# A four-stage convolution network: stack copies by quarter, a reordered opening, and six copies on GpSimd's queue

## The reference

```python
x = x + _L0_conv_ref(_gn(x), ...)   # 3x3 convolution, reflected edge; the kernel of each sample is a mix
                                    # of 3 experts, weighted by softmax(mean(_gn(x)) @ fc_w.T + fc_b)
x = x + _L1_conv_ref(_gn(x), ...)   # abs, then a 3x3 convolution per channel, zero edge
x = x + _L2_conv_ref(_gn(x), 8)     # 17x17 box mean, zero edge
x = x + _L3_conv_ref(_gn(x), ...)   # sum of the 8 neighbours, then five 1x1 layers, ELU after four of them
```

## Time and profile before

| | |
|---|---|
| median of 3 runs (lowest to highest) | 706.48 us (704.64 to 708.58) |
| profiled execution, its own time | 707.1 us |
| span of that execution, first to last instruction | 705.2 us |
| PE busy | 603.9 us, 86% of the span |
| DVE busy | 571.1 us, 81% |
| ACT busy | 558.4 us, 79% |
| POOL busy | 321.9 us, 46% |
| DMA | 85.54 MB, mean 121 GB/s |

### The profile page before, as it was taken

One profiled execution on the slowest core, in us unless ns is written; L12 is line 12 of the kernel. 1 busy time (PEld: TensorE's weight loads), 2 busy tenths in 40 slices (PEclk: granted clock), 3 DMA queues, 4 the chain that ended last, 5 costly groups with the idle time before them and its releaser, 6 DMA issues.

```text
span 705.2 us, 13422 instructions
## 1 busy us (share of the span) xinstructions
PE 603.9 (86%) x4142; PEld 167.3 (24%) x4142; DVE 571.1 (81%) x993; ACT 558.4 (79%) x1070; POOL 321.9 (46%) x487
## 2 busy tenths in 40 slices
PE   0547572999999999999999999999999899889995
PEld 0312220222222222222222222222222222222221
DVE  1454763888998899889988998988898779788896
ACT  0223101799999999999999999999999999999995
POOL 2530635146952696078717781579104910450000
PEclk9967886999999999999999999999999999999998
DMA  6779689338577737692869195728540750075001
GB/s 131 170 149 185 126 138 212 76 83 161 114 157 179 152 83 169 150 197 45 193 144 203 26 202 123 158 45 182 132 107 1 156 143 0 1 164 133 16 16 30
DMA packets 74418, 85.54 MB, mean 121 GB/s; under 512 B 9202, under 2 KB 58946, under 8 KB 74370
## 3 DMA queue, kind: packets, MB, share of 16 engines
q1 hardware_dynamic: 65976, 76.82, 50.3%
q10 hardware_dynamic: 8394, 8.12, 5.8%
HBM read 9.14 MB, written 8.39 MB: 25 GB/s over the span
## 4 chain that ended last, share of the span: by engine, by line
PE 46%; DVE 23%; ACT 14%; issue 8%; DMA 5%; SPq 2%; ACTq 1%; POOL 1%; DVEq 1%; POOLq 0%
PE pz L866 21%; PE pc L808 9%; DVE g L1073 8%; PE pc L843 7%; ACT u L719 6%; ACT u L722 5%; DVE bn L1015 4%; DVE g_last L1073 3%; PE po L808 3%; DMA win<-y 3%; PE po L875 2%; PE pz L843 2%; ACT u L725 2%; DVE u L1070 2%; DVE xs L1057 2%
## 5 line engine op out<-in xcount | busy, mean ns | idle before, releaser
L719 ACT ACTIVATE u<-pz 128x512 f32<-128x512 f32 x485 | 267.5, 602 | 67.7 <-PE pz L866 65.4
L866 PE MATMUL pz<-g,wT 64*64 64x512 f32 x1536 | 271.3, 610 | 17.7 <-DVE g L1073 15.7
L1073 DVE SCALAR_TENSOR_TENSOR g<-u,pz 128x512 f32<-128x512 f32 x384 | 246.8, 679 | 45.5 <-ACT u L722 42.1
L722 ACT ACTIVATE u<-u 128x512 f32<-128x512 f32 x485 | 282.6, 640 | 0.9
L866 PEld LDWEIGHTS pz<-g,wT 64*64 64x64 f32 x1536 | 69.3, 131 | 195.5 <-issue 194.1
L1073 DVE SCALAR_TENSOR_TENSOR g_last<-u,pz 128x512 f32<-128x512 f32 x128 | 82.4, 680 | 23.2 <-ACT u L722 22.2
L866 PE MATMUL pz<-stack,wT 64*64 64x512 f32 x512 | 86.3, 619 | 16.1 <-issue 9.6
L843 PE MATMUL pc<-win,t 64*32 64x512 f32 x1344 | 95.0, 639 | 4.9 <-DMA win<-y 2.0
L1015 DVE BATCH_NORM_STATS2 bn<-xs 128x6 f32<-128x512 f32 (+1 forms) x128 | 84.3, 683 | 15.7 <-DMA xs<-in_x_dram 13.1
L808 PE MATMUL pc<-box_sum,box_mat 128*128 128x512 f32 x138 | 74.5, 634 | 1.2 <-DVE box_sum L1089 0.8
L513 POOL TENSOR_TENSOR stat<-stat 128x1 f32<-128x1 f32 x32 | 6.2, 194 | 131.4 <-DVE stat L1030 131.4
(11 more groups left out here) (96 smaller groups left out, 480.5 us busy)
## 6 DMA issues: line engine op xcount, KB each, us to landing
stack<-near_sum SPq DMA_DIRECT2D x93, 192.0 KB, 4.0
win<-y SPq DMA_DIRECT2D x50, 260.0 KB, 4.4
win<-y SPq DMA_DIRECT2D x50, 195.0 KB, 4.4
stack<-box_sum SPq DMA_DIRECT2D x62, 128.0 KB, 3.9
out_dram<-xs SPq DMA_DIRECT2D x7, 1024.0 KB
xs<-in_x_dram SPq DMA_DIRECT2D x5, 1024.0 KB
stack<-near_sum SPq DMA_DIRECT2D x31, 128.0 KB, 2.8
win<-y SPq DMA_DIRECT2D x25, 65.0 KB, 4.5
```

What stands on the lines that cost most here:

```text
L719: act.activation(u[:, m, :], pz[:, m, :], ACT.Relu, scale=-1.0, bias=0.0).then_inc(relu_done, 1)
L722: act.activation(u[:, m, :], u[:, m, :], ACT.Exp, scale=-1.0).then_inc(exp_done, 1)
L866: last = pe.matmul(pz[to, m, :], wT[rows, l, rows], src, start=True, stop=True)
L1073: dve.scalar_tensor_tensor(out=elus(l)[:, m, :], in0=u[:, m, :], scalar=-1.0, in1=pz[:, m, :], op0=ALU.add, op1=ALU.max).then_inc(g_writte ...
```

## The change

The opening is put in another order, and some waits are split.

- The stack of sample 0 goes by quarters (`stack_chunks`, `own_pieces`, `near_pieces`). SP and ACT copy the own rows of quarter 0 as soon as `y3` is written, its neighbour rows after the first neighbour sum, then the own rows of the other three quarters, then the neighbour rows of quarter 1; SP then copies the neighbour rows of the second half. Quarter 0 counts to `stack_first`, the other own rows to `own_first`, the rest to `stack_in`, whose later thresholds become lower by `OWN` or are shifted by it. The layer of quarter 0 waits for `stack_first` alone.
- The first half of sample 2's stage-0 convolution moves on PE from half-step 0 of round 1 to the end of the opening, into `pz[0..1]`, with its evacuation and statistics on DVE; the second half is spread over half-steps 1, 2 and 3, its evacuation moves to half-step 4. The first layer waits for that evacuation.
- Both halves of sample 2's load are issued by SP, after the first windows have landed.
- Sample 1's windows of stage 0: SP copies the upper half after the first half of sample 0's convolution, and the last pieces after the second. The six copies of the lower half are issued by POOL, behind `scales(0, 1)` and ahead of `scales(2, 0)`, and count to `win0_second`. ACT does `normal0(1, c)` ahead of `softmax_exp(1)`.
- DVE does `route_out(0)` ahead of `setup_transposed`.

```diff
win0_in = sem("win0_in")
+        win0_second = sem("win0_second")
...
         stack_in = [sem(f"stack_in{h}") for h in range(2)]
+        stack_first = sem("stack_first")
+        own_first = sem("own_first")
...
         WIN0 = 14 * 16
+        SECOND = 6 * 16
...
         STACK = 14 * 16
+        OWN = 4 * 16
...
-            first = {(0, 0, 1): 2, (0, 1, 0): 0, (1, 0, 1): 2, (1, 1, 0): 2}
+            first = {(0, 0, 1): 2, (0, 1, 0): 0, (1, 0, 1): 2, (1, 1, 0): 2, (2, 0, 0): 0}
...
-        def written(eng, k, h):
-            eng.wait_ge((y0_written, y1_written)[k], (Y0, Y1)[k] // 2 * (h + 1))
+        def windows0_next(eng):
+            eng.wait_ge(conv_mm[0], 1)
+            windows0(eng, 1, (0,), False)
+            eng.wait_ge(y0_written, 2 * Y0)
+            eng.wait_ge(conv_mm[0], 2)
+            for h in range(2):
+                for dst, rows in around(y0, win0, h * K // 2, (h + 1) * K // 2, h, True):
+                    eng.dma_start(dst, rows).then_inc(win0_in, 16)
+        def written(eng, k, h, i=0):
+            n = (Y0, Y1)[k]
+            eng.wait_ge((y0_written, y1_written)[k], n * i + n // 2 * (h + 1))
...
+        def near_pieces(eng, lo, hi, banks, landed):
+            up, down, end = max(lo, 1), lo and lo - (lo > KB), min(hi, K - 1) - (hi == 2 * KB)
+            for m in banks:
+                a, b = max(2 * m - 1, 0), min(2 * m + 3, R)
+                top, bottom = C * (a - 2 * m + 1), C * (b - 2 * m)
+                eng.dma_start(stack[m][top:3 * C, lo:hi], near_sum[C * a:C * (2 * m + 2), lo:hi]).then_inc(landed, 16)
+                eng.dma_start(stack[m][5 * C:5 * C + bottom, lo:hi], near_sum[2 * C * m:C * b, lo:hi]).then_inc(landed, 16)
+            if 0 in banks:
+                eng.dma_start(stack[0][0:C, up:hi], near_sum[7 * C:P, up - 1:hi - 1]).then_inc(landed, 16)
+            if M - 1 in banks:
+                if lo == 0:
+                    eng.wait_ge(near_rows, 2)
+                eng.dma_start(stack[3][7 * C:P, down:end], near_sum[0:C, down + 1:end + 1]).then_inc(landed, 16)
+        def own_pieces(eng, lo, hi, banks, landed):
+            for m in banks:
+                eng.dma_start(stack[m][3 * C:5 * C, lo:hi], y3[2 * C * m:2 * C * m + 2 * C, lo:hi, 1:W + 1]).then_inc(landed, 16)
+        def stack_chunks(eng, banks):
+            eng.wait_ge(y3_written, 4)
+            own_pieces(eng, 0, KB, banks, stack_first)
+            eng.wait_ge(near_rows, 1)
+            near_pieces(eng, 0, KB, banks, stack_first)
+            own_pieces(eng, KB, K, banks, own_first)
+            eng.wait_ge(near_rows, 2)
+            near_pieces(eng, KB, 2 * KB, banks, stack_in[0])
...
             windows_first(sp, 0, 2, True)
-            load_blocks(sp, 2, 0)
-            sp.wait_ge(conv_mm[0], 2)
-            windows0(sp, 1, (0,), True)
+            for h in range(2):
+                sp.wait_ge(win0_first[h], FIRST0)
+            for odd in range(2):
+                load_blocks(sp, 2, odd)
+            windows0_next(sp)
...
             load(3)
-            stacks(sp, 0, 0, (0, 1))
-            stacks(sp, 0, 1, range(M))
+            stack_chunks(sp, (0, 1))
+            sp.wait_ge(near_rows, Q)
+            near_pieces(sp, 2 * KB, K, range(M), stack_in[1])
...
                     pool.wait_ge(norm_step[0], i * NORM + NORM)
-                    pool.wait_ge(win0_in, WIN0 * (i - 1))
+                    pool.wait_ge(win0_in, WIN0 * (i - 1) - SECOND)
...
-                if c == 0:
+                if c == 0 and not (isinstance(i, int) and i == 0):
                     for h in range(2):
-                        pool.wait_ge(stack_in[h], STACK * i)
+                        pool.wait_ge(stack_in[h], STACK * i - OWN)
+                    if isinstance(i, int) and i == 1:
+                        pool.wait_ge(stack_first, STACK)
...
             scales(0, 1)
+            pool.wait_ge(conv_mm[0], 2)
+            written(pool, 0, 1, 1)
+            for dst, rows in around(y0, win0, K // 2, K, 1, False) + [edge0(1)]:
+                pool.dma_start(dst, rows).then_inc(win0_second, 16)
...
                             act.wait_ge(win0_first[h], FIRST0)
-                    elif not (isinstance(i, int) and i == 0):
-                        act.wait_ge(win0_in, WIN0 * (i - 1))
+                    elif isinstance(i, int) and i == 2:
+                        act.wait_ge(win0_in, WIN0 - SECOND)
+                        act.wait_ge(win0_second, SECOND)
...
             windows_first(act, 0, 3, True)
-            load_blocks(act, 2, 1)
-            softmax_exp(1)
...
                 normal0(1, c)
-            act.wait_ge(conv_mm[0], 2)
-            windows0(act, 1, (1,), False)
+            softmax_exp(1)
...
             windows1(act, 1, (1,), False)
-            stacks(act, 0, 0, (2, 3))
+            stack_chunks(act, (2, 3))
...
                             pe.wait_ge(setup_dve, SETUP_DVE)
+                    elif isinstance(i, int) and (i, k, n) == (2, 0, 0):
+                        pe.wait_ge(conv_evac[2], 2)
+                    elif isinstance(i, int) and (i, k, n) == (2, 0, 1):
+                        pe.wait_ge(conv_evac[1], Q * i)
...
                     elif n == 0:
-                        pe.wait_ge((win0_in, win1_in)[k], (WIN0, WIN1)[k] * i)
+                        pe.wait_ge((win0_in, win1_in)[k], (WIN0 * i - SECOND, WIN1 * i)[k])
+                        if isinstance(i, int) and i == 1 and k == 0:
+                            pe.wait_ge(win0_second, SECOND)
...
                         if isinstance(j, int) and j == 0 and q == 0 and m % 2 == 0:
-                            pe.wait_ge(conv_evac[2 - m // 2], (2, Q + 2)[m // 2])
-                        if m == 0 and q < 2:
-                            pe.wait_ge(stack_in[q], STACK * j + STACK)
+                            pe.wait_ge(conv_evac[m // 2], (2 * Q + 2, Q + 2)[m // 2])
+                        if m == 0 and q == 0 and isinstance(j, int) and j == 0:
+                            pe.wait_ge(stack_first, STACK)
+                        elif m == 0 and q == 0:
+                            pe.wait_ge(stack_in[0], STACK * (j + 1) - OWN)
+                        elif m == 0 and q == 1:
+                            if isinstance(j, int) and j == 0:
+                                pe.wait_ge(own_first, OWN)
+                                pe.wait_ge(stack_in[0], STACK - OWN)
+                            pe.wait_ge(stack_in[1], STACK * (j + 1) - OWN)
...
                                     conv_taps(t + 1, 1, n, (kw,))
-                                if first and at in (0, 2):
-                                    conv_taps(t + 1, 0, at // 2, range(3))
+                                if first and at in (1, 2, 3):
+                                    conv_taps(t + 1, 0, 1, (at - 1,))
...
             conv_taps(1, 1, 1, range(3))
+            conv_taps(2, 0, 0, range(3))
...
                         dve.wait_ge(conv_mm[2], Q * i)
-                        for h in range(2):
-                            dve.wait_ge(stack_in[h], STACK * i)
+                        if isinstance(i, int) and i == 1:
+                            dve.wait_ge(stack_first, STACK)
+                            dve.wait_ge(own_first, OWN)
+                        else:
+                            for h in range(2):
+                                dve.wait_ge(stack_in[h], STACK * i - OWN)
...
                 if first:
-                    if at in (0, 2):
-                        evacuate_pair(i, 0, at // 2)
-                    if at in (1, 4):
-                        stats_of(i, 1, (0, 2) if at == 1 else (1, 3))
                     if at == 4:
+                        evacuate_pair(i, 0, 1)
+                        stats_of(i, 1, (1, 3))
...
             setup_natural()
+            route_out(0)
             setup_transposed()
-            route_out(0)
...
             merge_stats(1, 2)
+            evacuate_pair(2, 0, 0)
             group_var(1, 2)
+            stats_of(2, 1, (0, 2))
...
             rounds(dve, one)
```

## The result

| | before | after |
|---|---|---|
| median of 19 runs each (lowest to highest) | 706.48 us (702.87 to 710.62) | 710.86 us (708.32 to 713.46) |
| span of the profiled execution | 705.2 us | 707.7 us |
| ratio of the runs, 95% interval | | 1.0058 (1.0044 to 1.0072) |

The account below looks back on a forecast made before the run. The kernel's end was taken as its pipeline's start plus a constant, so opening time counts. Part 1's 8.9 plus 0.7 for part 2 and Part 3 gave 9.6 off 707.1, 697.5, less 0.6: 696.9 us, range 691 to 702.5.

Parts of the forecast that it names:

- part 2: Opening, first windows and routing: first convolution's second half at 36.35, sample 0's second normalisation 2.34 earlier; with Part 3, 0.7 us.
- The later load of sample 2: Opening: sample 2's load, issued after the first windows land, costs nothing; a landing at 53 would cost three us.
- a gain at the first windows: Sample 0's first convolution: last window copy lands in 3.1 instead of 7.38 us, at 34.3 instead of 38.55.
- Part 3: Six copies on GpSimd, 1.14 us each, end at 53.7; sample 1's convolution at 56.8; with part 2, 0.7 us.
- Copies that land 3.1 after their issue are in by then: Sample 1's window copies land before its convolution starts at 56.8, so they don't hold it.
- the six copies end last: Sample 1's windows: copies share DMA with 2.1 MB of second-stage windows, land at 59 to 62; 699 to 702; chance 0.16.
- Part 1: Stack by quarters: layer on banks 2 and 3 starts 10.2 us earlier, less 2.5 for clock, plus 1.2: 8.9 us.
- only SP's part is late for it, and I take 110: First quarter of the stack: sample 3's load, in SP's queue, delays only SP's copies; landing at 110.
- the quarter lands late: Stack: sample 3's load holds SP's part, ACT's fourteen smaller copies keep it issuing; landing at 115, 701 us; chance 0.08.
- The low clock behind the gap: TensorE behind its gap between 109 and 115: possible 1.2 GHz clock costs 0 to 4.4 us, taken as 2.5.
- the signs of being wrong: GpSimd copies over 2 us, first layer still released by a copy, or first round longer by what the opening saved.
- The slower rival, VectorE holding up GpSimd: Sample 1's six GpSimd copies: each held 2.5 us, convolution 14.8 late, 711.9 us; chance 0.06.

Follow-up runs that it names:

- experiment 1: Changed kernel, but sample 1's six copies issued by ScalarE behind its softmax of sample 1 instead of by GpSimd: 709.11 us, 1.0027 to the kernel before.
- experiment 2: Changed kernel, but GpSimd issues its six copies ahead of sample 1's mixing: 707.95 us, 1.0027 to the kernel before.
- experiment 3: Changed kernel, but sample 2's load back in its old place, half SP, half ScalarE; copies left on GpSimd: 707.33 us, 1.0020 to the kernel before.
- experiment 4: Changed kernel with sample 2's load in its old place and the six copies on ScalarE behind softmax: 700.69 us, 0.9899 to the kernel before.
- experiment 5: Changed kernel with sample 2's load in its old place and GpSimd's six copies ahead of its mixing: 703.68 us, 0.9966 to the kernel before.
- experiment 6: Kernel before with only the stack by quarters and the first half of sample 2's convolution moved as in the change: 702.54 us, 0.9930.
- experiment 8: experiment 6 with the second half of sample 2's convolution whole at half-step 0, its evacuation at 2: 702.29 us, 0.9918 to the kernel before.
- experiment 10: experiment 4 with the second half of sample 2's convolution whole at half-step 0, its evacuation at 2: 700.67 us, 0.9930 to the kernel before.
- experiment 9: experiment 6 with the edits of experiment 7 and experiment 8 together: 698.18 us, 0.9867 to the kernel before.
- experiment 7: experiment 6 with sample 3's load issued ahead of sample 1's second-stage windows on SP: 703.53 us, 0.9941 to the kernel before.

## Why the prediction was wrong

**The step that failed** is in part 2: "The later load of sample 2 has until some 50 before its statistics hold anything up, and I cost it at nothing; a landing at 53 would cost three." The step asked when the load's own reader needs it, and on that it came near: the statistics began at 49.91. It did not ask which transfers the load meets, and the load met all copies of sample 1's windows. The same part books a gain at the first windows, a landing of 3.1 in place of 7.38 us because the load no longer goes out right behind them, and charges nothing to the next windows, which it now goes out ahead of. Experiments 1 and 2 show the copies late on each queue with the load there; experiments 3 and 4 show that it takes part in a loss of which neither half can be taken back alone. With the copies on ScalarE it costs 9.0 us (experiments 1 and 4).

**Part 3** had the issue right and the landing wrong. An issue on GpSimd took 0.50 to 0.77 us, below the 1.14 taken, and the last ended at 50.1, not 53.7. That the logits came near their forecast all the same (57.78 for 56.8) is luck: GpSimd had won 3.6 us with its short issues, and lost 4.2 again waiting for sample 2's statistics, late with their load. "Copies that land 3.1 after their issue are in by then" was the fault: that median came from a stretch in which most copies were out before the load was; the one that ran beside it took 7.38. The rival "the six copies end last" named this mechanism, with landings at 59 to 62 and 2 to 5 us lost, and set against it that these copies start first. They landed at 64.55, and the convolution was 8.0 behind the forecast: the rival counted the 2.1 MB of second-stage windows but not the load before them. Without that load the last piece took 8.26 beside the same windows (experiment 3), not 14.94.

The Trainium skill, "DMA: Bandwidth & Descriptors", section "Issuing engines are not separate DMA queues", says that a third issuer saves issue time only, and was given as the rule behind that rival. The runs agree: GpSimd's copies land in 5.7 to 6.9 in free company (experiment 5) and ScalarE's in 5.4 to 7.0 (experiment 4), and with the load in their way in 8.8 to 18.5 (experiment 2) and 7.9 to 14.3 (experiment 1); in both of these the last of sample 1's window copies is in at 61.

**Part 1** was mis-sized: 4.3 (the stretch behind `y3` in the change, and the time of experiment 6) for 8.9. Single traces scatter: in the nine that have the stack by quarters and sample 3's load in its place, that stretch is 1.0 to 6.0 shorter than before, in none 8.9. Its premise held, since the end of the kernel is the second quarter's layer plus a constant. The term that was off is the landing: "only SP's part is late for it, and I take 110", with `y3` at 96.88; in the change `y3` is at 103.43 and the landing at 121.94, so 18.5 behind it instead of 13.1. The load of sample 3 shares the engines with ScalarE's part too (147 to 171 GB/s in experiment 6, for the 207 taken), and it holds back SP's first issue and VectorE's statistics. The rival "the quarter lands late" had it, with a landing at 115, 18.1 behind `y3`, and 701. The low clock behind the gap is there as expected: three layers at 1.98. The new wait at half-step 5 had not been foreseen; taking it away alone brought nothing (experiments 8 and 10), and together with the load's move it went along with some 4.4 us (experiment 9). Of the signs of being wrong that the prediction named, one came: a first layer still released by a copy.

**Right** were the second half of the first convolution (36.11 for 36) and ScalarE's second normalisation (46.54 for 47); its 12 issues that follow, and SP's, are what met the six copies. Whether this reordering is worth something by itself is not shown: experiment 4 is 1.85 us below experiment 6, which has the old order, but their intervals overlap. The slower rival, VectorE holding up GpSimd, did not come about: no issue was over 0.77 us. In the change VectorE was idle beside them until 49.91; in experiments 2 and 5 it had evacuations and statistics there, and no issue was over 0.78. No run has these copies beside a scan. The kernel is slower for another reason than the one priced there.

The sum: 8.0 at the convolution (of which 7.25 are left at `y3`), and 4.6 at the stack, make 11.8 of the 12.1 us between the span as forecast, 705.2 - 9.6, and the 707.7 measured; the other 0.3 lie behind the second quarter's layer (561.7 to 562.0).

**Left open:** the load of sample 3 was only moved between two places that both hold copies. Whether some place costs nothing was not found. How much of the lateness of SP's copies comes from standing behind the load in SP's own queue, and how much from sharing the engines with it, no run separates: none issues the load at that time from another queue. ScalarE's and GpSimd's copies, late without a load in their queue, show that sharing has a part.

## What to carry to other kernels

A transfer that is moved has to be costed against the transfers that it will run beside, not only against the first reader of its own data; take the landing time from rows in equal company, and the joint rate of such a mix from a stretch that has it. If moving a transfer away from some copies is booked as a gain, book the loss for the copies it is moved to. Where two late copies end at the same moment, undo both before either is acquitted: alone they gave 2.2 and 2.7 us, together 11.2. Look at what a wait does to the granted clock behind it: 48 multiplications that brought nothing behind a long wait went with 4.45 us of the trace where they filled a gap of 3 us. And when an engine is given copies because it is idle, look at what stands ahead of them in its order and what then stands behind them.

## What was unexpected of the hardware

- A load and copies together, at a full share, move little more than the load alone: 114 to 158 GB/s at a DMA share of 1.03 to 1.05 in the change from 40 to 48, with 100 at a share of 0.62 for a load. Copies alone move 175 to 236 in the stretches shown.
- Even a piece of 8 KB is under way for 14.94 us beside the second-stage windows, after the load had held up the copies before it, and for 8.26 beside the same windows without that load (experiment 3).
- A first copy that stands behind a load of 1 MB in SP's queue takes 3.42 us to issue (experiment 6); two of them take 1.32 together where the load is out of the queue (experiment 7).
- The second half of the first convolution, which no longer waits for its windows, ran at the full clock throughout: 2.81 us, in place of 4.57 behind the gap, at a granted clock of 1.00, 2.4 GHz, from 36 to 40.
